# Turning quantised activations and weights by DMA instead of on TensorE in a fused patch-embedding, attention and feed-forward layer

## Chip, cores and metric

The kernel runs on one core of one Trainium2 chip. The metric is the device time of one execution in microseconds (us). A "turn" below is the transposition of a 128 x 768 bf16 tile as six blocks of 128 x 128.

## The reference

The reference takes 64 images of 49 patches with 768 values each and does three things.

1. Tokens: each patch row is RMS-normalised and quantised to 8-bit integers, multiplied by a ternary weight (768 to 256), and a class token and a position vector are added: `h` is 64 x 50 x 256.
2. Attention: the layer norm of `h` goes through three attention passes of 16 heads of width 16, each with its own q, k, v and output weights, a causal mask, a softmax and a layer norm. Their outputs are joined, projected to 256, normalised and added to `h`.
3. Feed-forward: the layer norm of `h` is quantised with one scale for the whole tensor, multiplied by 8-bit gate and up weights (256 to 704), `silu(gate) * up` is quantised again and multiplied by the 8-bit down weight.

```python
xn = patches * rsqrt(mean(patches**2) + 1e-6)
s  = 127.0 / clip(max(abs(xn)), 1e-5)
proj = einsum('bnd,od->bno', clip(round(xn * s), -128, 127) / s, ternary(weight))
```

## The kernel before

The 64 images are worked on in 8 groups (`GROUPS`) of 8 images, each as 4 pairs (`PAIRS`) of two images. Pairs are counted through, n = 0 to 31. One pair fills 128 partitions: one image in rows 0 to 63, the other in rows 64 to 127.

A pair's way to the token matmul is a chain over the engines. SP loads the two images into one of two buffers `x_in` (step `sums` on SP). ACT and DVE take the sum of squares and the largest value (`sums`), DVE makes the scale (`scale`). ACT writes the scaled and shifted values to `x_t`, and DVE subtracts the constant and writes bf16 integers to `x_q` (`shift`, L1083). TensorE turns `x_q` with six 128 x 128 transpositions into a PSUM bank (`turn_q`, L1287), ACT copies the bank to `x_qT` (`turn_q`, L746), and TensorE multiplies `x_qT` by the token weight in six matmuls (`embed`, L1296). DVE scales the product into `hidden` (`embed`, L1104). `x_q` and `x_qT` are single buffers.

Four more units ("chunks" 0 to 3, n = 32 to 35) bring the gate and up weights of the feed-forward stage along the same way during the last group: they are loaded into `x_in`, quantised through `x_t` into `x_q`, turned on TensorE and copied by ACT into `wgT` (L743). Two more chunks hold the down weight, and are turned in another place.

The rest of a group is attention. TensorE makes k and q (L1314) and v (`v`, L1330 and L1333), the scores in 12 units a group (`scores`, L1349 and L1358), turns the probabilities (`turn_p`, L1373), multiplies them by v (`heads`, L1383) and projects (`project`, L1394 and L1399). Most of these go through four PSUM banks `ps_w` used in turn: a step waits until the step four fills earlier has been read.

The order of all steps is written out by hand in the table `AT`. It lists for each engine at which position it does step number i of a kind. Each engine walks its list in that order and waits on semaphores inside a step. PE has 594 steps, ACT 637, DVE 813, POOL 457 and SP 41. Groups overlap: pairs of the next group are embedded while the attention of this one runs. What counts as the position of a step below is its number in its engine's list.

After the attention comes the feed-forward stage, which has its own fixed loops.

Of the kernel before, what the change touches and what calls it, by code (L numbers as in the profile page):

```python
# [32 lines left out]
P = 128  # L33
# [40 lines left out]
    "act": {  # L74
        "sums": (0, 1, 10, 11, 25, 26, 51, 54, 99, 100, 117, 125, 176, 178, 195, 200, 250, 256, 268, 278, 324, 326,
            342, 346, 401, 402, 429, 439, 481, 482, 501, 504,),
        "shift": (2, 5, 13, 15, 33, 39, 61, 71, 106, 113, 137, 145, 185, 188, 205, 213, 260, 266, 283, 289, 332, 338,
            356, 362, 407, 419, 451, 466, 490, 495, 511, 528, 563, 568, 595, 618,),
        "tok_shift": (3,),
        "turn_q": (4, 9, 16, 19, 43, 55, 69, 82, 110, 129, 140, 156, 189, 209, 221, 232, 265, 277, 292, 298, 337,  # L80
            358, 367, 376, 421, 445, 460, 471, 496, 508, 527, 538, 577, 593, 611, 635,),
        "tok_copy": (6, 7,),
        "q_hi": (8,),
        "k_hi": (12,),
        "v_cut": (14, 18, 36,),
        "small": (17,),
        "wv_hi": (20,),
        "turn_x": (21, 22, 23, 24, 93, 95, 97, 98, 170, 171, 172, 173, 244, 246, 247, 248, 319, 321, 322, 323, 397,
# [23 lines left out]
        "fold_hi": (57, 62, 63,),  # L112
        "y_spread": (64,),
        "heads": (67, 70, 89, 90, 118, 135, 139, 158, 159, 167, 196, 206, 220, 227, 239, 240, 271, 279, 301, 307,
            314, 318, 351, 357, 372, 381, 389, 395, 420, 438, 447, 458, 459, 468, 498, 518, 519, 536, 537, 546, 576,
            582, 599, 600, 612, 620, 626, 633,),
        "project": (73, 76, 80, 84, 101, 115, 116, 124, 126, 127, 138, 147, 148, 149, 164, 165, 166, 174, 175, 201,
# [1680 lines left out]
```

## Time and profile before

| | |
|---|---|
| median of 3 runs | 771.42 us (769.8 to 774.2) |
| profiled execution, its own time | 769.84 us |
| its span | 768.1 us |
| busy: PE, DVE, ACT, POOL | 89%, 84%, 76%, 68% of the span |
| token set-up and first group's start | 0 to about 48 us |
| attention stage | about 48 to 660 us |
| hand-over and feed-forward stage | about 660 to 768 us |

Busy time of TensorE counts modelled ends of pipelined matmuls, so a busy engine isn't at its peak; what an operation costs there is read from the distance of one start to the next. Waits are inferred from semaphore events. The windows of the profile give the busy time of each engine in a stretch of the span.

### The profile page before, as it was taken

What the parts mean: (1) busy time and instruction counts of PE and PEld (TensorE: products, weight loads), DVE (VectorE), ACT (ScalarE), POOL (GpSimd) and SP (SyncE); (2) the same over time, 40 slices, a digit from 0 to 9 for tenths busy, and PEclk for the clock granted to TensorE, in tenths of its full rate; (3) what the DMA queues carried; (4) which work ended last, traced back from release to release, by engine and by line L of the source; (5) the groups of instructions that cost most, each with busy time, mean ns of one, the idle gap of its engine ahead of it and who ended that gap; (6) DMA issues with size and microseconds to landing.
All of it is one profiled execution on the core that took longest, in us unless ns stands there. A gap on an engine that the chain in (4) does not pass through costs nothing. (4 is left out here: it accounts for less than half of the span.)

```text
span 768.1 us, 25770 instructions
## 1 busy us (share of the span) xinstructions
PE 684.5 (89%) x9862; PEld 535.2 (70%) x9862; DVE 641.9 (84%) x1395; ACT 584.3 (76%) x1280; POOL 520.0 (68%) x793
## 2 busy tenths in 40 slices
PE   0498799999999999999999999999999999568866
PEld 0277678777877787877877787788778777334455
DVE  4788876899889988989898899889987898759947
ACT  3567888687788678869778878688868887379875
POOL 3459965957687859877677789478948786521154
PEclk9979999999999999999999999999999999869979
DMA  8301000000000000101000000100100000000005
GB/s 240 100 28 33 17 19 17 19 18 20 4 32 27 10 2 34 34 2 33 18 19 3 16 19 3 34 18 18 41 3 22 20 22 22 1 1 1 0 24 148
DMA packets 14980, 21.95 MB, mean 29 GB/s; under 512 B 1992, under 2 KB 11466, under 8 KB 14860
## 3 DMA queue, kind: packets, MB, share of 16 engines
q1 hardware_dynamic: 14424, 19.91, 8.4%
q8 instruction: 80, 1.31, 0.7%
q10 hardware_dynamic: 436, 0.40, 0.4%
q14 instruction: 40, 0.33, 0.1%
HBM read 17.03 MB, written 3.28 MB: 26 GB/s over the span
## 5 line engine op out<-in xcount | busy, mean ns | idle before, releaser
L905 POOL TENSOR_TENSOR k_bd<-kT,rmask 128x400 f32<-128x400 f32 x192 | 167.8, 902 | 7.5 <-PE ps_s L1358 4.3
L806 ACT COPY pT<-ps_w 25x400 f32<-25x400 f32 x192 | 94.8, 494 | 9.2 <-PE ps_w L1373 6.7
L1399 PE MATMUL ps_w<-oy_hi,o_hi 128*128 128x512 f32 x192 | 94.9, 494 | 0.0
L914 POOL TENSOR_TENSOR prob_hi<-prob_hi,rsum 128x800 f32<-128x800 f32 x48 | 74.9, 1559 | 13.3 <-DVE rsum L1151 13.3
L1134 DVE TENSOR_REDUCE nmax<-ps_s 128x16 f32<-128x400 f32 x96 | 72.4, 765 | 11.6 <-PE ps_s L1358 11.3
L786 ACT COPY v_bd<-ps_w 50x256 f32<-50x256 f32 x192 | 70.4, 367 | 13.2 <-PE ps_w L1333 10.9
L1399 PE MATMUL ps_w<-oy_hi,o_lo 128*128 128x512 f32 x192 | 76.3, 397 | 0.0
L1399 PE MATMUL ps_w<-oy_lo,o_hi 128*128 128x512 f32 x192 | 76.2, 397 | 0.0
L827 ACT ACTIVATE ps_w<-ps_w 128x256 f32<-128x256 f32 x96 | 35.6, 371 | 51.7 <-PE ps_w L1399 50.3
L1358 PE MATMUL ps_s<-k_bd,qT 64*25 64x200 f32 (+1 forms) x3072 | 70.5, 291 | 0.0
L919 POOL TENSOR_TENSOR ln<-ln,ln_eps 128x1 f32<-128x1 f32 x96 | 19.9, 208 | 74.6 <-ACT ps_w L827 74.1
L1314 PE MATMUL ps_w<-xh_dense,qk_hi 128*128 128x400 f32 x192 | 68.5, 357 | 1.5 <-DVE xl L1126 1.1
L1314 PE MATMUL ps_w<-xl,qk_hi 128*128 128x400 f32 x192 | 67.2, 350 | 0.0
L1314 PE MATMUL ps_w<-xh_dense,qk_lo 128*128 128x400 f32 x192 | 66.2, 345 | 0.0
L1333 PE MATMUL ps_w<-wv_hi,xh 128*128 128x256 f32 x192 | 61.9, 322 | 0.0
L921 POOL TENSOR_TENSOR ln<-ln,neg_half 128x1 f32<-128x1 f32 x96 | 54.4, 567 | 7.5
L914 POOL TENSOR_TENSOR prob_lo<-prob_lo,rsum 128x400 f32<-128x400 f32 x48 | 42.5, 886 | 19.5 <-DVE rsum L1151 19.5
L1373 PE MATMUL ps_w<-pack,prob_hi 128*128 128x128 f32 x384 | 51.7, 277 | 2.9 <-DVE acc L1169 1.0
L1333 PE MATMUL ps_w<-wv_lo,xh 128*128 128x256 f32 x192 | 54.0, 281 | 0.0
L1333 PE MATMUL ps_w<-wv_hi,xl 128*128 128x256 f32 x192 | 53.7, 280 | 0.0
L1373 PEld LDWEIGHTS ps_w<-pack,prob_hi 128*128 128x128 f32 x384 | 42.1, 141 | 11.1 <-issue 6.5
L813 ACT COPY pT<-ps_w 128x400 f32<-128x400 f32 x96 | 43.3, 506 | 8.1 <-PE ps_w L1373 7.3
(237 smaller groups left out, 2070.4 us busy)
## 6 DMA issues: line engine op xcount, KB each, us to landing
x_in<-in_x SPq DMA_DIRECT2D x64, 147.0 KB
out<-hidden SPq DMA_DIRECT2D x14, 200.0 KB
pT<-in_tok_w SPq DMA_DIRECT2D x1, 768.0 KB, 6.5
hidden<-in_wq SPq DMA_DIRECT2D x1, 768.0 KB, 8.6
k_bd<-in_wk SPq DMA_DIRECT2D x1, 768.0 KB, 9.5
v_bd<-in_wv SPq DMA_DIRECT2D x1, 768.0 KB, 9.2
hidden<-in_wout SPq DMA_DIRECT2D x1, 768.0 KB, 9.3
hidden<-in_wo SPq DMA_DIRECT2D x1, 768.0 KB, 10.8
```

Source lines behind the costliest of these rows:

```text
L786: last = nc.scalar.copy(v_bd[row:row + L, s % 2, b::2, :, e * HD:(e + 1) * HD], v_ps[src:src + L, :, e])
L806: last = nc.scalar.copy(pT[ROWB * h:ROWB * h + LQ, s % 2, c::2, :, 0:LQ], ps_w[row:row + LQ, bank].rearrange("p (j t) -> p j t", j=4)[:, : ...
L813: nc.scalar.copy(pT[:, s % 2, 4 * a:4 * a + 4, :, LQ:L], ps_w[:, bank].rearrange("p (j t) -> p j t", j=4)[:, :, 0:QB * LQ].rearrange("p j ...
L905: last = nc.gpsimd.tensor_tensor(k_bd[:, v % KBD, c], kT[:, w % 2, c, 2 * p * L:(2 * p + 2) * L].unsqueeze(1).broadcast_to([P, HR, 2 * L]) ...
L914: nc.gpsimd.tensor_tensor(pr, pr, rsum[:, s % 2, e].unsqueeze(2).broadcast_to([P, H, WIDTH[e]]), ALU.mult).then_inc(prob_ready, 1)
L921: nc.gpsimd.tensor_tensor(ln2[:, v, 2:3], ln2[:, v, 1:2], neg_half[:, 0:1], ALU.pow).then_inc(r2_ready, 1)
L1134: nc.vector.tensor_reduce(top, s_ps, AX.X, ALU.max, negate=True).then_inc(max_ready, 1)
L1314: mm = nc.tensor.matmul(G[:, 0:GT], wt[:, w, q, k, c * P:(c + 1) * P], xt[:, k, :, 0:L], start=(t == 0), stop=(t == 3 * KC - 1))
L1333: mm = nc.tensor.matmul(cols, xt[:, k, two].rearrange("p b t -> p (b t)"), wt[:, w, k], start=False, stop=(k == KC - 1 and xt is xl))
L1358: mm = nc.tensor.matmul(ps_s[32 * b:32 * b + LQ, e, r, c * HR * W:(c + 1) * HR * W], qT[rows, w % 2, c, first:first + LQ], k_bd[rows, v % ...
L1373: mm = nc.tensor.transpose(G[:, j * P:(j + 1) * P], flat[:, (4 * a + j) * P:(4 * a + j + 1) * P], pack[:])
L1399: mm = nc.tensor.matmul(G[:], ot[:, s % 2, c, 2 * (p % 2):2 * (p % 2) + 2].rearrange("p b t -> p (b t)"), wt[:, w, c], start=False, stop=( ...
```

## The change

For pairs 4 to 31 and for weight chunks 0 to 3 (n = 32 to 35), the six transpositions on TensorE and the copy on ACT go away. SP has a new kind of step, `turn_d`: it waits until `x_q` is written and, for a pair, until the token matmul of the pair before has read `x_qT`. Then it issues six DMAs with `transpose=True`, each of which turns 128 x 128 bf16 from `x_q` in SBUF straight into `x_qT` (pairs) or `wgT` (chunks). All count up one semaphore `xqT_turned`, 16 each. The next `shift` on DVE and the token matmul on TensorE wait for the full count of all six. The four pairs of the first group are turned on TensorE and copied by ACT as before.

The table `AT` is new for every engine: PE has 562 steps (32 fewer), ACT 605 (32 fewer), DVE 813, POOL 457 and SP 73 (32 more). Steps of all kinds have other positions.

```diff
@@ AT @@
     "sp": {
-        "sums": (0, 1, 5, 6, 7, 8, 9, 10, 11, 12, 13, 14, 15, 16, 17, 18, 19, 20, 21, 22, 23, 24, 25, 26, 27, 28, 29,
-            30, 31, 32, 33, 34, 35, 36, 37, 38, 39, 40,),
-        "weights": (2, 3, 4,),
+        "sums": (0, 1, 4, 5, 7, 8, 10, 11, 14, 15, 17, 19, 23, 24, 25, 27, 31, 32, 34, 35, 38, 39, 42, 43, 45, 48,
+            49, 51, 55, 56, 58, 59, 62, 63, 65, 67, 70, 71,),
+        "weights": (2, 3, 6,),
+        "turn_d": (9, 12, 13, 16, 18, 20, 21, 22, 26, 28, 29, 30, 33, 36, 37, 40, 41, 44, 46, 47, 50, 52, 53, 54, 57,
+            60, 61, 64, 66, 68, 69, 72,),
     },
...
@@ pe @@
-        "turn_q": (1, 3, 8, 10, 29, 41, 58, 67, 94, 108, 123, 138, 167, 185, 197, 206, 241, 252, 264, 272, 308, 326,
-            334, 346, 387, 411, 424, 436, 459, 467, 489, 499, 538, 552, 571, 591,),
+        "turn_q": (1, 3, 7, 9,),
-        "embed": (5, 6, 9, 12, 40, 48, 64, 73, 102, 118, 135, 152, 170, 189, 203, 214, 246, 256, 267, 286, 322, 331,
-            345, 356, 390, 423, 435, 439, 463, 475, 496, 504,),
+        "embed": (5, 6, 8, 11, 34, 42, 53, 73, 97, 107, 118, 139, 163, 185, 198, 208, 231, 252, 267, 275, 300, 313,
+            328, 345, 370, 382, 404, 409, 436, 446, 464, 481,),
...
@@ sync @@
             def do(step):
                 kind, m = step[0], step[-1]
+                if kind == "turn_d":
+                    n = PAIRS + step[1]
+                    c = ffn_chunk(n // PAIRS, n % PAIRS)
+                    sp.wait_ge(xq_ready, n + 1)
+                    if c is None:
+                        bank, fill = bank_of(("embed", (n - 1) % PAIRS, (n - 1) // PAIRS))
+                        sp.wait_ge(filled[bank], fill)
+                        dst = x_qT[:]
+                    else:
+                        dst = wgT[:, c // 2, 3 * (c % 2):3 * (c % 2) + 3].rearrange("p f k t -> p (f k) t")
+                    for j in range(PC):
+                        sp.dma_start(dst[:, j], x_q[:, j * P:(j + 1) * P], transpose=True).then_inc(xqT_turned, 16)
...
             for b in (0, 1):
                 sp.wait_ge(x_loaded[b], 64 * GROUPS + 96)
+            sp.wait_ge(xqT_turned, 16 * PC * PAIRS * GROUPS)
...
@@ scalar, turn_q @@
-                    c = ffn_chunk(m, p)
-                    if c is not None:
-                        w_ps = ps_w[:, bank, 0:PC * P // 2].bitcast(BF16)
-                        dst = wgT[:, c // 2, 3 * (c % 2):3 * (c % 2) + 3].rearrange("p f k t -> p (f k t)")
-                        nc.scalar.copy(dst, w_ps).then_inc(xqT_ready, 1)
-                        return
...
@@ vector, shift @@
-                    need(dve, xqT_ready, n)
+                    need(dve, xqT_ready, min(n, PAIRS))
+                    need(dve, xqT_turned, 16 * PC * (n - PAIRS))
...
@@ tensor, embed @@
-                    pe.wait_ge(xqT_ready, PAIRS * m + p + 1)
+                    if m == 0:
+                        pe.wait_ge(xqT_ready, p + 1)
+                    else:
+                        pe.wait_ge(xqT_turned, 16 * PC * (PAIRS * (m - 1) + p + 1))
```

## Rows read from the trace of the kernel before

**Rows 1.** The page's first part: busy time, share and instructions of each engine.

```profile
PE 684.5 (89%) x9862; PEld 535.2 (70%) x9862; DVE 641.9 (84%) x1395; ACT 584.3 (76%) x1280; POOL 520.0 (68%) x793
```

**Rows 2.** Windows: stretch, length, busy time (instructions) by engine, clock, DMA share, GB/s.

```profile
276.00:352.00 76.00, 75.33 (x1171) 60.91 (x1170) 66.60 (x157) 61.90 (x146) 59.49 (x99) 1.00 0.06 18
...
504.00:580.00 76.00, 74.48 (x1167) 60.25 (x1166) 67.75 (x157) 59.51 (x140) 57.20 (x92) 1.00 0.07 20
...
sum 612.00, PE 590.52 PEld 475.60 DVE 530.77 ACT 487.02 POOL 464.82; mean PE 73.81 PEld 59.45 DVE 66.35 ACT 60.88 POOL 58.10
```

**Rows 3.** Windows from 660 us to the end of the span, same columns.

```profile
660.00:674.00 14.00, 4.94 (x14) 3.30 (x14) 9.43 (x29) 1.69 (x6) 7.18 (x19) 0.77 0.00 0
674.00:768.00 94.00, 68.76 (x470) 43.92 (x470) 70.97 (x95) 73.14 (x134) 29.79 (x29) 0.88 0.13 36
```

**Rows 4.** Timeline of PE, 299 to 318 us: start, length, instructions merged.

```profile
299.89 0.92 PE L1383 MATMUL ps_w<-pT,v_bd 128*32 128x50 f32 x64
300.74 0.66 PE L1373 MATMUL ps_w<-pack,prob_lo 128*128 128x128 f32 x4
...
311.42 0.51 PE L1287 MATMUL ps_w<-id,x_q 128*128 128x128 bf16 x6
311.77 1.04 PE L1373 MATMUL ps_w<-pack,prob_hi 128*128 128x128 f32 x8
312.65 0.27 PE L1330 MATMUL ps_w<-bias,ones 96*128 96x256 bf16 x1
...
314.32 0.83 PE L1296 MATMUL ps_w<-tokT,x_qT 128*128 128x256 bf16 x6
314.98 0.60 PE L1373 MATMUL ps_w<-pack,prob_lo 128*128 128x128 f32 x4
...
316.21 1.09 PE L1373 MATMUL ps_w<-pack,prob_hi 128*128 128x128 f32 x8
317.23 0.27 PE L1349 MATMUL ps_s<-mask,pick 64*128 64x200 bf16 x2
```

**Rows 5.** Groups by line, ACT's copies: busy us, mean ns, idle before.

```profile
L746 ACT COPY x_qT<-ps_w 128x768 bf16<-128x768 bf16 x32 | 25.5, 797 | 4.8 <-DVE ln L1107 4.1 <-PE ps_w L1287 0.4
...
L743 ACT COPY wgT<-ps_w 128x768 bf16<-128x768 bf16 x4 | 3.2, 803 | 0.7 <-PE ps_w L1287 0.7
```

**Rows 6.** Waits of PE, 50 to 650 us: total us, times, longest.

```profile
PE ps_s L1349 <- DVE prob_lo L1138: 1.8, 1, 1.8
...
PE ps_w L1330 <- ACT x_qT L746: 1.4, 1, 1.4
```

**Rows 7.** Line L1287 as an instruction group: ns min/median/max, starts, forms.

```profile
L1287 PE MATMUL ps_w<-id,x_q x216: 216/219/314, 16.8 to 659.7; 128*128 128x128 bf16 x108
```

**Rows 8.** Timeline of DVE: the `shift` of n = 4 and of n = 35.

```profile
60.76 1.21 DVE L1083 TENSOR_SCALAR x_q<-x_t 128x768 bf16<-128x768 f32 x1
...
645.53 0.55 DVE L1083 TENSOR_SCALAR x_q<-x_t 128x768 bf16<-128x768 f32 x1
```

**Rows 9.** DMA issue on SP, 100 to 600 us: ns min/median/max of one.

```profile
L631 SPq DMA_DIRECT2D x_in<-in_x x44: 268/271/845, 131.4 to 519.1; - x44
```

**Rows 10.** Issues on SP at the start: start, length, and one's us to landing.

```profile
4.06 0.63 SPq L607 DMA_DIRECT2D hidden<-in_head_mask  x1
...
id<-in_ident SPq DMA_DIRECT2D x1, 64.0 KB, 7.2
```

**Rows 11.** Windows of 1 us behind the `x_q` that ended at 308.8 us.

```profile
308.00:309.00 1.00, 1.00 (x7) 0.96 (x6) 0.97 (x4) 0.69 (x3) 0.33 (x2) 1.00 0.00 0
309.00:310.00 1.00, 1.00 (x8) 1.00 (x7) 1.00 (x2) 1.00 (x3) 0.92 (x3) 1.00 0.21 31
310.00:311.00 1.00, 1.00 (x7) 1.00 (x6) 1.00 (x3) 1.00 (x2) 1.00 (x2) 1.00 0.33 123
311.00:312.00 1.00, 1.00 (x13) 0.83 (x12) 1.00 (x4) 1.00 (x3) 1.00 (x2) 1.00 0.43 164
312.00:313.00 1.00, 1.00 (x11) 0.99 (x10) 0.87 (x4) 1.00 (x3) 1.00 (x2) 1.00 0.00 0
```

**Rows 12.** Waits of SP's queue over the span.

```profile
SPq L631 <- DVE x_q L1083: 480.9, 29, 43.5
```

More of the change, by code:

```diff
@@ L73 @@
     },
     "act": {
[L75 to L81, printed above, removed]
@@ L112 @@
[L112 to L117, printed above, removed]
[4 rows of a table removed]
+        "sums": (0, 1, 10, 11, 26, 27, 42, 48, 93, 94, 118, 120, 166, 167, 186, 188, 239, 244, 257, 260, 307, 313,
+            332, 340, 383, 385, 403, 408, 453, 459, 472, 478,),
@@ new lines @@
+        "tok_shift": (2,),
+        "shift": (3, 5, 14, 15, 31, 36, 49, 77, 101, 110, 127, 135, 172, 177, 199, 212, 247, 253, 279, 289, 321, 330,
+            346, 365, 388, 395, 425, 430, 464, 469, 484, 502, 530, 539, 550, 567,),
+        "small": (4,),
+        "turn_q": (6, 12, 16, 17,),
+        "tok_copy": (7, 8,),
+        "q_hi": (9,),
+        "k_hi": (13,),
+        "v_cut": (18, 20, 37,),
+        "wv_hi": (19,),
+        "turn_x": (21, 23, 24, 25, 89, 90, 91, 92, 161, 162, 163, 164, 232, 234, 235, 238, 303, 304, 305, 306, 378,
+            380, 381, 382, 448, 449, 451, 452, 520, 521, 523, 527,),
@@ new lines @@
+        "wo_hi": (35,),
+        "soft": (43, 44, 50, 51, 63, 64, 69, 70, 85, 97, 103, 104, 111, 112, 122, 124, 132, 133, 143, 145, 156, 158,
[4 rows of a table added]
+        "y_spread": (47,),
+        "z_cut": (53, 65, 71,),
+        "v": (54, 55, 66, 73, 86, 87, 136, 137, 147, 148, 159, 160, 206, 208, 218, 220, 229, 233, 271, 272, 286, 287,
+            301, 302, 350, 351, 358, 359, 375, 379, 419, 420, 431, 440, 441, 450, 495, 496, 503, 509, 517, 518, 553,
+            558, 579, 583, 593, 594,),
+        "turn_p": (56, 57, 58, 62, 74, 75, 79, 82, 108, 109, 116, 117, 128, 129, 138, 141, 144, 149, 150, 151, 181,
[4 rows of a table added]
@@ L122 @@
+        "fold_hi": (60, 67, 72,),
+        "heads": (61, 68, 83, 84, 114, 123, 139, 146, 155, 157, 184, 194, 210, 211, 228, 231, 261, 263, 280, 285,
+            299, 300, 333, 338, 354, 355, 368, 376, 402, 410, 424, 432, 439, 447, 470, 487, 500, 501, 514, 516, 540,
+            557, 566, 574, 582, 592, 595, 602,),
+        "project": (76, 78, 80, 81, 88, 95, 96, 119, 121, 130, 131, 134, 142, 152, 153, 154, 165, 178, 179, 192, 195,
[4 rows of a table added]
     },
     "pool": {
-        "sums": (0, 1, 3, 4, 12, 13, 28, 32, 55, 57, 69, 75, 111, 112, 126, 127, 166, 167, 179, 186, 219, 220, 232,
-            234, 275, 277, 301, 305, 334, 335, 345, 359,),
@@ new lines @@
+        "embed": (4, 5, 9, 10, 33, 50, 52, 53, 93, 99, 100, 104, 129, 147, 160, 161, 192, 197, 216, 218, 250, 253,
+            263, 277, 294, 318, 324, 325, 357, 378, 380, 381,),
+        "k_lo": (6,),
+        "v_left": (7, 15,),
+        "turn_x": (8, 16, 32, 42, 49, 55, 75, 78, 119, 154, 157, 158, 191, 193, 196, 200, 273, 274, 304, 305, 311,
+            331, 347, 352, 375, 395, 411, 412, 427, 434, 435, 445,),
+        "spread": (13, 14, 17, 18, 19, 20, 25, 30, 36, 37, 41, 51, 60, 61, 64, 65, 66, 69, 70, 85, 86, 87, 97, 98,
[4 rows of a table added]
@@ L159 @@
[L159 to L163 removed]
+        "tok_sum": (0,),
+        "sums": (1, 3, 12, 13, 32, 33, 45, 63, 115, 116, 143, 144, 213, 214, 235, 239, 314, 322, 332, 339, 408, 416,
+            437, 449, 509, 510, 535, 540, 605, 610, 630, 639, 694, 714, 715, 742, 796, 797,),
@@ L164 @@
+        "tok_unit": (2,),
+        "scale": (4, 5, 14, 15, 34, 35, 48, 90, 119, 125, 150, 162, 217, 222, 246, 260, 321, 327, 338, 358, 414, 419,
+            448, 460, 513, 514, 557, 567, 611, 622, 633, 659,),
+        "id_cast": (6,),
+        "shift": (7, 9, 17, 19, 37, 44, 59, 91, 123, 133, 159, 171, 219, 230, 259, 284, 323, 330, 371, 381, 418, 433,
+            457, 485, 517, 529, 568, 579, 618, 627, 654, 674, 712, 721, 750, 789,),
         "tok_clip": (8,),
         "consts": (10,),
-        "embed": (11, 16, 23, 26, 60, 69, 93, 102, 138, 159, 182, 209, 229, 260, 277, 291, 334, 349, 366, 385, 437,
-            451, 468, 482, 532, 580, 594, 598, 626, 644, 674, 683,),
@@ L214 @@
-        "sig": (499,),
+        "embed": (11, 16, 20, 23, 53, 65, 80, 102, 138, 155, 172, 203, 233, 267, 287, 298, 333, 361, 385, 396, 428,
+            453, 476, 497, 533, 550, 585, 589, 631, 643, 671, 693,),
+        "q_lo": (18,),
+        "o_centre": (21,),
+        "norm_x": (22, 25, 26, 28, 97, 105, 106, 107, 200, 201, 202, 206, 295, 297, 300, 303, 383, 392, 399, 400,
+            487, 496, 500, 503, 591, 593, 596, 597, 677, 690, 691, 696,),
+        "y_row": (24,),
+        "x_lo": (27, 29, 30, 31, 108, 110, 113, 114, 207, 209, 210, 211, 301, 307, 309, 312, 401, 402, 403, 405, 504,
+            505, 506, 507, 599, 600, 603, 604, 695, 697, 699, 706,),
@@ new lines @@
+        "b_centre": (36,),
+        "wv_lo": (38,),
+        "max": (39, 41, 46, 47, 66, 67, 71, 74, 89, 100, 111, 112, 129, 131, 139, 140, 157, 158, 173, 177, 189, 194,
[4 rows of a table added]
+        "soft": (40, 42, 49, 50, 68, 69, 78, 79, 96, 101, 120, 121, 130, 132, 142, 146, 160, 161, 176, 180, 191, 197,
[4 rows of a table added]
+        "y_scale": (43,),
+        "bo_col": (51,),
+        "sum": (52, 57, 60, 61, 75, 76, 82, 83, 103, 122, 126, 127, 134, 135, 151, 152, 163, 170, 178, 184, 199, 205,
[4 rows of a table added]
+        "z_row": (54, 55,),
+        "over": (56, 58, 62, 64, 77, 84, 85, 86, 104, 124, 128, 136, 141, 145, 153, 154, 165, 179, 181, 185, 204,
[4 rows of a table added]
@@ new lines @@
+        "o_lo": (70,),
+        "fold_lo": (72, 81, 88,),
+        "heads": (73, 87, 98, 99, 137, 149, 174, 186, 196, 198, 234, 247, 272, 274, 294, 299, 340, 342, 368, 373,
+            393, 394, 438, 445, 469, 470, 483, 499, 532, 542, 563, 573, 586, 595, 626, 649, 666, 667, 684, 688, 722,
+            746, 754, 765, 780, 794, 795, 804,),
+        "project": (92, 93, 94, 95, 109, 117, 118, 147, 148, 164, 166, 168, 182, 192, 193, 195, 216, 226, 227, 245,
[4 rows of a table added]
+        "mix": (156, 167, 169, 183, 254, 262, 263, 275, 350, 356, 357, 379, 452, 459, 464, 465, 553, 554, 565, 584,
[3 rows of a table added]
@@ L215 @@
+        "sig": (511,),
     },
@@ new lines @@
+        "beta": (10,),
+        "wo_turn": (12, 17, 45,),
+        "turn_x": (13, 14, 15, 16, 74, 78, 79, 80, 143, 144, 145, 147, 209, 213, 214, 215, 278, 279, 282, 283, 348,
[7 rows of a table added]
+        "scores": (24, 25, 31, 32, 41, 46, 49, 52, 58, 60, 76, 77, 91, 92, 99, 100, 109, 110, 120, 121, 127, 131,
[4 rows of a table added]
+        "bo_turn": (33,),
+        "y_spread": (35,),
+        "bo_fold": (37, 38,),
+        "v": (39, 40, 54, 59, 71, 72, 115, 116, 128, 129, 140, 141, 183, 184, 192, 195, 206, 210, 245, 246, 258, 259,
+            276, 277, 320, 321, 326, 327, 343, 347, 385, 386, 395, 406, 407, 413, 456, 457, 465, 469, 479, 480, 512,
+            517, 536, 541, 550, 551,),
@@ new lines @@
+        "turn_p": (43, 44, 47, 51, 61, 62, 65, 68, 90, 93, 98, 101, 108, 111, 117, 123, 125, 130, 132, 133, 158, 161,
[4 rows of a table added]
+        "fold": (48, 56, 57,),
+        "heads": (50, 55, 69, 70, 95, 104, 119, 126, 137, 138, 164, 171, 189, 190, 204, 207, 236, 237, 255, 256, 273,
+            274, 304, 306, 324, 325, 337, 344, 366, 376, 389, 396, 405, 412, 432, 449, 462, 463, 476, 477, 503, 518,
+            525, 533, 540, 549, 553, 559,),
+        "project": (63, 64, 66, 67, 75, 81, 82, 102, 103, 112, 113, 114, 124, 134, 135, 136, 148, 155, 156, 169, 172,
[4 rows of a table added]
@@ L264 @@
     "mix": PAIRS, "mix2": PAIRS, "k": NS * KC, "q": NS * KC, "v": S, "heads": S, "spread": V, "project": V,
-    "scores": U, "max": U, "soft": U, "sum": U, "over": U, "turn_p": U,
+    "kbd": S, "scores": U, "max": U, "soft": U, "sum": U, "over": U, "turn_p": U,
 }
```

96 lines of the change are left out of this document (15 added, 81 removed), and 138 rows, old and new, of the table AT.

## The prediction

> **What bounds the kernel now.** I read the page's shares first, then windows of the length of a group, then the waits of the fullest engine, then its timeline around one turn. The shares alone put TensorE first with 89% and DVE second with 84% [rows 1]. The windows show that the mean hides a stage where TensorE is full: in two windows of 76 us, about a group each, it is busy for 75.33 and 74.48 us, with DVE at 66.60 and 67.75 and ACT at 61.90 and 59.51, at a granted clock of 1.00 [rows 2]. Over eight such windows (48 to 660 us) it is busy for 590.52 of 612 us, so 21.5 us are idle [rows 2]. Each wait that remains in this stage is short: the longest is 1.8 us, and one of 1.4 us was for ACT's copy of a turned tile [rows 6]. So in this stage the end is set by the sum of TensorE's work, and each slot taken off TensorE should shorten it. What follows, 660 to 768 us, is another stage that is not touched, except that it needs `wgT`; there TensorE is busy 4.94 of 14 us and 68.76 of 94 us [rows 3].
>
> **What goes from TensorE.** A turn is six transpositions. Each lasts 219 ns by its record [rows 7], but they overlap: six start at 311.42 and the next step starts at 311.77, a slot of 0.35 us [rows 4]. The records' lengths would give 0.51 us a turn [rows 4]; I take the distance of starts, 0.34 to 0.35 us, since a modelled end lies under the next step's start. 28 pairs and 4 chunks make 32 turns, and 32 x 0.34 = 10.9 us. The upper bound is 32 x 0.51 = 16.3 us.
>
> The Trainium skill (VectorE: DVE Perf Modes, section "The three transpose paths") gives 390 ns for a 128 x 128 bf16 transposition on TensorE and 1309 ns for one by DMA. By its first figure 192 transpositions would give back 75 us, an estimate from that page; the rows disagree with it, as six take 0.35 us in a full stream. By its second figure, six in a row would take an estimated 7.9 us, which is taken up among the rivals.
>
> **What goes from ACT.** 28 copies of 0.797 us and 4 of 0.803 us, 25.5 us in all [rows 5]. ACT has some 15 us free in each window of 76 [rows 2], so this is worth nothing by itself. It lets ACT empty banks sooner, and each bank is filled 32 times less in total. The one PE wait that names the copy is 1.4 us [rows 6], and I take that. Bounds: nothing, and a third of TensorE's idle 21.5 us, 7 us [rows 2].
>
> **What is added.** SP issues 192 more DMAs. SP mostly waits: 480.9 us of its time went to waiting for `x_q` before a load [rows 12]. So its own time costs nothing, but what it does between `x_q` and the token matmul does. Call T the time from the end of `shift` to the landing of all six. No row shows a transposing DMA. From below: six issues at the 0.27 us of a plain load [rows 9], 1.6 us, and 1 us until something lands, so about 2.7 us; behind the `x_q` that ended at 308.8 us the bytes of the next load (2 x 147 KB) flow from 309 to 312 us [rows 11], 3 us for 294 KB against the 192 KB of a turn, so bytes are no obstacle. From above: six issues at 0.63 us, the longest of the small loads at the start, and the 7.2 us to landing of a 64 KB load among many [rows 10], 11 us. At neither end does a stage like this stand: the queue is nearly empty here (share 0.06) [rows 2], which draws it to the lower end, and turning may cost more issue and more transfer than copying, which draws it up. I take 6 us.
>
> **What waits for a turn.** Behind a late turn stand the token matmul on TensorE, with every later step of its list, and the next `shift` on DVE, with every later step of that list. What cover has a turn? DVE's steps from `shift` of n = 4 (position 42 before, start 60.76) to that of n = 35 (position 788, 645.53) take 584.8 / 746 = 0.78 us each [rows 8]. In the new lists DVE has k steps between `shift` of a pair and its own `embed` step, which must come after TensorE's. Taken off are about 0.6 us for the `shift` itself and 0.9 us for the matmuls, so the cover is 0.78k - 1.5. The smallest k are 10 (n = 16, 20, 27), 11 (7), 12 (23), 13 (10, 28), 14 (12, 15, 18), 15 (8, 19) and 16 (4, 24, 29); 10 gives 6.3 us, 11 gives 7.1, 12 gives 7.9 and 13 gives 8.7. The chain of `x_qT` has a cover too: `turn_d` of n waits for the matmul of n - 1, and between the token matmuls of 26 and 27 the new list has only `heads`, two `v` and one `turn_p`. With 0.85, 2 x 1.67 and 1.02 us by the distances of starts [rows 4] that is 5.2 us. The next smallest are 7.4 us (18 to 19), 7.5 (4 to 5) and 8.3 (5 to 6) by the same sort of sum. On SP's list a load of two images stands just ahead of some turns and is set free by the same `x_q`: of those above before n = 7, 8, 12, 19, 24 and 29. Its 3 us of bytes [rows 11] overlap the six issues, so I add 2 us to T for these.
>
> Stalls by T then:
> - T = 6: n = 27 lacks 0.8 us, n = 7 (8 against 7.1) 0.9 us; 1.7 us in all.
> - T = 8: n = 16 and 20 lack 1.7 each, 27 2.8, 7 2.9, 12 0.5, 19 0.6, 5 0.5; about 11 us.
> - T = 9: about 21 us.
> - T = 11: 16 and 20 4.7 each, 27 5.8, 7 5.9, 12 3.5, 5 3.5, 23 3.1, 8 and 19 2.8 to 3.6 each, and eight smaller ones; about 51 us.
>
> So the decision lies near T = 8 us.
>
> Loads move too. A load behind a `turn_d` in SP's list is kept until that turn is issued; the shortest distance to the step that reads it is 9 DVE steps (7 us) for n = 15, 18 and 19, and 3 for chunk 34, against 3 us of bytes and up to 3.8 us of issues [rows 10, 11]. DVE then loses up to 2 us near the end once, and has over 8 us free in each window [rows 2]; nothing. At the end, `turn_d` of n = 35 is the last step on SP; its `shift` has 23 steps behind it on DVE, some 18 us, which hides T.
>
> **Sum.** -10.9 (TensorE) - 1.4 (bank wait) + 1.7 (stalls at T = 6) = -10.6 us. From the profiled execution's own 769.84 us that is 759.2; it stands 1.6 us under the median of the runs, 771.42, which gives 760.8. I predict 761 us.
>
> **Rivals.** What can be told from no change is 0.5%, about 3.9 us: 767.6 to 775.3 us.
>
> - Turning fits its cover (T up to 7.3 us), forecast: 753 to 767 us. For it: TensorE without waits, a nearly empty DMA queue. Chance 0.60.
> - The gain is used up: T of 7.3 to 8.5 us, or the new lists leave some 8 us more idle time on TensorE in places that have nothing to do with turning (the 21.5 us are 2.7 a window, and every step has been moved; DVE, busy 67 of 76 us, has little room to catch up). 769.84 - 10.9 + 8 is 767, on the median 769; 768 to 775 us. Chance 0.16.
> - Slower, one mechanism: the six DMAs don't overlap, so that each adds its own whole turn to T. With 1.5 us each T is 9, and 21 us of stalls less 12.3 give +9, 780 us; at 11 us it is +39, 810 us. It decides from 1.4 us each. For it: nothing in the trace shows a turning DMA, and small ones pay mostly a fixed cost (0.27 us of issue for a load and 0.63 us for one of 4 KB [rows 9, 10]). Against it: the loads' issues overlap their bytes [rows 11]. The skill's 1309 ns, if the six follow one another, puts an estimated 7.9 us at the very point of decision, a stall of some 10 us and an estimated time of about 770. Chance of a slower kernel 0.24.
> - That the change doesn't do what it says: the transpositions do go from TensorE's list, so this has no chance of its own.
>
> **Range.** The low end is the 10.9 us and the 7 us of idle time given back, 753 us on the median. The high end takes in T = 9 us, 780 us, and 2 us for the lists, 782 us; above it are T over 9 us, about 0.13, and below 753 about 0.05. The likeliest case alone has 753 to 767 us. Faster 0.60, within 0.5% 0.16, slower 0.24.
>
> **What the new profile would show.** L1287 only 24 times on PE, L746 4 times, L743 gone. Six issues per turn on SP: at 0.3 to 0.5 us each the forecast holds, at over 1 us it fails. T between 5 and 7 us. The waits of PE: the token matmul of n = 27 and of n = 7 among the few waits for a DMA, below 3 us in total. TensorE busy in the windows of the attention stage as fully as now, 97 to 98%, with the stage 10 to 12 us shorter, and the feed-forward stage as long as now, about 94 us. The prediction is wrong if the waits for `x_qT` add up to over 5 us, if many PE waits on other engines grow, or if the slot of a turn wasn't 0.34 us in most places.

## The result and the profile after

| | before | after |
|---|---|---|
| median | 770.79 us (4 runs, 769.8 to 774.2) | 819.61 us (4 runs, 815.17 to 826.21) |
| ratio, 95% interval | | 1.0632 [1.054, 1.0724] |
| profiled execution, span | 769.84, 768.1 us | 815.17, 813.4 us |

The change makes the kernel 49 us slower. The forecast was 761 us, 753 to 782.

I read the page first: busy time by engine, the granted TensorE clock in 40 slices, and the DMA packets.

```profile
PE 693.8 (85%) x9670; PEld 538.8 (66%) x9670; DVE 650.8 (80%) x1395; ACT 562.0 (69%) x1248; POOL 518.6 (64%) x793
...
PEclk9979999999999999999899999898999999959979
...
DMA packets 45701, 28.26 MB, mean 35 GB/s; under 512 B 32712, under 2 KB 42186, under 8 KB 45580
```

The 192 matmul records of the turns are gone (9862 to 9670, [rows 1]), yet every engine has a smaller share of a longer span. The clock has slices of 8 in the middle. Then the windows, to find the stage:

```profile
48.00:648.00 600.00, 548.43 (x8128) 438.22 (x8128) 488.18 (x1085) 419.17 (x966) 418.54 (x641) 0.96 0.11 28
...
276.00:352.00 76.00, 69.49 (x1050) 56.45 (x1050) 64.98 (x143) 53.81 (x127) 54.26 (x88) 0.96 0.13 35
504.00:580.00 76.00, 65.94 (x940) 51.67 (x940) 56.97 (x135) 47.27 (x112) 49.33 (x83) 0.91 0.11 28
719.00:813.40 94.40, 69.59 (x470) 44.31 (x470) 70.99 (x95) 73.23 (x134) 29.79 (x29) 0.86 0.13 36
```

The last row answers to the last of [rows 3]: the feed-forward stage still takes 94 us. So all of the loss lies in the attention stage, which ends at about 705 us in place of 660. In the windows of [rows 2] TensorE was busy for 75.33 and 74.48 us at a clock of 1.00; now it is 69.49 us at 0.96 and 65.94 us at 0.91. The waits of 50 to 700 us name what is late:

```profile
POOL ln L927 <- ACT ps_w L835: 103.7, 56, 8.7
ACT ps_w L835 <- PE ps_w L1411: 55.4, 53, 5.9
PEld ps_w L1308 <- DMA x_qT<-x_q: 36.5, 16, 5.2
PE ps_w L1308 <- DMA x_qT<-x_q: 32.3, 15, 4.8
DVE x_q L1092 <- DMA x_qT<-x_q: 23.0, 8, 4.5
```

The same two first rows of the kernel before, 50 to 660 us:

```profile
POOL ln L919 <- ACT ps_w L827: 69.5, 48, 7.6
ACT ps_w L827 <- PE ps_w L1399: 45.7, 50, 2.1
```

The token matmul (L1308) waits 32.3 us in 15 pairs for its turn and the next `shift` (L1092) 23.0 us in 8. I had named a sum over 5 us as what would refute the forecast. The largest waits of the token matmul were 4.8 us at n = 20, 4.3 at 23, 3.9 at 28 and 3.4 at 16. POOL and ACT had long waits in the kernel before too; they are 34 and 10 us longer now, in turn, for what TensorE does late. Why a turn takes so long is in the issue rows of SP's queue (ns min/median/max):

```profile
L616 SPq DMA_TRANSPOSE x_qT<-x_q x168: 1093/1232/2590, 54.5 to 609.6; - x168
L616 SPq DMA_TRANSPOSE wgT<-x_q x24: 1093/1233/2695, 628.6 to 699.8; - x24
```

A load held the queue for 0.27 us [rows 9]; a transposing DMA holds it for 1.23 us, and the six of a turn stand in one queue. The timeline of one turn, n = 8, on SP, DVE and PE:

```profile
134.26 0.62 SPq L644 DMA_DIRECT2D x_in<-in_x  x2
134.97 8.54 SPq L616 DMA_TRANSPOSE x_qT<-x_q  x6
...
133.60 0.62 DVE L1092 TENSOR_SCALAR x_q<-x_t 128x768 bf16<-128x768 f32 x1
...
144.73 1.46 PE L1308 MATMUL ps_w<-tokT,x_qT 128*128 128x256 bf16 x6 [2.99 <-DMA x_qT<-x_q]
```

`x_q` is ready at 134.22. The load takes 0.7 us, six issues 8.54 us, and the matmul that waits for the last starts 1.2 us later: T is 10.5 us. Without a load ahead it is shorter: at n = 10 `x_q` is ready at 163.67 and the waiting token matmul starts at 172.38, so T is 8.7 us; at n = 16 and n = 20 it is 9.6 and 9.7 us.

A wait has a second price. At n = 16 TensorE stands still from 301.4 to 304.75 us; here is PE's timeline, and then windows of 1 us:

```profile
304.75 1.12 PE L1308 MATMUL ps_w<-tokT,x_qT 128*128 128x256 bf16 x6 [3.35 <-DMA x_qT<-x_q]
305.67 1.06 PE L1385 MATMUL ps_w<-pack,prob_lo 128*128 128x128 f32 x4
```

```profile
303.00:304.00 1.00, 0.00 (x0) 0.00 (x0) 0.00 (x0) 0.00 (x0) 0.00 (x0) 1.00 0.15 33
...
306.00:307.00 1.00, 1.00 (x7) 1.00 (x6) 0.29 (x1) 0.00 (x0) 0.00 (x0) 0.50 0.51 192
307.00:308.00 1.00, 1.00 (x6) 1.00 (x5) 0.51 (x1) 0.51 (x1) 0.00 (x0) 0.50 0.49 95
308.00:309.00 1.00, 1.00 (x37) 0.48 (x35) 0.88 (x4) 0.99 (x4) 0.31 (x1) 0.72 0.42 160
```

From 303 to 304 us no engine works. When TensorE runs again, its clock is at 1.2 GHz (0.50) for about 3 us: the six matmuls take 1.12 us and the four behind them 1.06 us, where they took 0.83 and 0.60 to 0.66 us at 2.4 GHz [rows 4].

### The profile page after: what moved, and what is told of

It is laid out like the page before. It is cut to its first block and busy times, and to the rows that moved or that the text cites. A ratio compares the mean times of both kernels' runs of the same rounds, so it can differ in the third digit from the quotient of the medians.

```text
span 813.4 us, 25514 instructions
## 1 busy us (share of the span) xinstructions
PE 693.8 (85%) x9670; PEld 538.8 (66%) x9670; DVE 650.8 (80%) x1395; ACT 562.0 (69%) x1248; POOL 518.6 (64%) x793
## 5 line engine op out<-in xcount | busy, mean ns | idle before, releaser
L913 POOL TENSOR_TENSOR k_bd<-kT,rmask 128x400 f32<-128x400 f32 x192 | 164.8, 887 | 6.0 <-ACT kT L774 4.7
L814 ACT COPY pT<-ps_w 25x400 f32<-25x400 f32 x192 | 94.6, 492 | 12.3 <-PE ps_w L1385 10.0
L1370 PE MATMUL ps_s<-k_bd,qT 64*25 64x200 f32 (+1 forms) x3072 | 72.8, 296 | 1.5 <-issue 1.5
L1326 PE MATMUL ps_w<-xh_dense,qk_hi 128*128 128x400 f32 x192 | 70.2, 366 | 1.2 <-DVE xl L1135 0.8
L1308 PE MATMUL ps_w<-tokT,x_qT 128*128 128x256 bf16 x192 | 32.5, 316 | 37.7 <-DMA x_qT<-x_q 32.3
L1385 PE MATMUL ps_w<-pack,prob_hi 128*128 128x128 f32 x384 | 54.6, 287 | 4.8 <-DVE acc L1178 3.4
L1385 PEld LDWEIGHTS ps_w<-pack,prob_hi 128*128 128x128 f32 x384 | 45.1, 147 | 13.5 <-issue 5.5
```

Source lines behind the costliest of these rows:

```text
L814: last = nc.scalar.copy(pT[ROWB * h:ROWB * h + LQ, s % 2, c::2, :, 0:LQ], ps_w[row:row + LQ, bank].rearrange("p (j t) -> p j t", j=4)[:, : ...
L913: last = nc.gpsimd.tensor_tensor(k_bd[:, v % KBD, c], kT[:, w % 2, c, 2 * p * L:(2 * p + 2) * L].unsqueeze(1).broadcast_to([P, HR, 2 * L]) ...
L1326: mm = nc.tensor.matmul(G[:, 0:GT], wt[:, w, q, k, c * P:(c + 1) * P], xt[:, k, :, 0:L], start=(t == 0), stop=(t == 3 * KC - 1))
L1370: mm = nc.tensor.matmul(ps_s[32 * b:32 * b + LQ, e, r, c * HR * W:(c + 1) * HR * W], qT[rows, w % 2, c, first:first + LQ], k_bd[rows, v % ...
L1385: mm = nc.tensor.transpose(G[:, j * P:(j + 1) * P], flat[:, (4 * a + j) * P:(4 * a + j + 1) * P], pack[:])
```

## The experiments

All runs are single-core, each with runs of the kernel before on the same chip; "before" is their median (770.8 to 772.4 us). They fall into two questions. First: what makes a turn slow, its bytes, its number of DMAs, or the lists? Second, once that was known: where are the 10.9 us that TensorE was to save?

### The number of DMAs in a turn (e1, e2, e5, e6)

e1 issues only the first of six DMAs for each pair (five sixths of `x_qT` keep old values), e2 the first four (a third keeps old values); chunks keep all six.

```diff
-for j in range(PC):
+for j in range(1 if c is None else PC):     # e1; 4 in e2
```

> The changed kernel, but of each pair's turn only the first of the six DMAs is issued for pairs 4 to 31 (so five of six blocks of x_qT keep old data; the weight chunks are turned whole). In the changed kernel one transposing DMA keeps SP's queue for 1.23 us (median of 168) and a turn takes 9 to 10.5 us from x_q to the token matmul. Theory A (the length of a turn is the cause: waits of TensorE for x_qT, 32.3 us, and stretches at half clock behind them): a turn takes 2.5 to 3 us here, no wait for x_qT is left, no half clock in the attention stage, and the time is 757 to 764 us. Theory B (the new lists of steps are themselves worse): still over 785 us. Theory C (turning DMAs slow the other engines by using SBUF beside them): a part of the loss stays in proportion to the DMAs, about a sixth of 48 us, 8 us, so 767 to 772 us.

> As e1, with four of the six DMAs for each pair (two blocks keep old data). A turn should take about 4 x 1.3 + 1.2 = 6.4 us, close to the 6 us that the prediction took. Theory A: the prediction's table of stalls gives 2 to 4 us for it, so 761 to 766 us, waits of TensorE for x_qT below 4 us. Theory B: over 785 us. Theory C: two thirds of the 48 us stay, about 800 us.

e5 turns the same data as one DMA of 128 x 768, and e6 as twelve of 64 x 128.

```diff
-for j in range(PC):
-    sp.dma_start(dst[:, j], x_q[:, j * P:(j + 1) * P], transpose=True).then_inc(xqT_turned, 16)
+sp.dma_start(dst, x_q[:], transpose=True).then_inc(xqT_turned, 16)                                  # e5
+for j in range(PC):                                                                                 # e6
+    for r in (0, 64):
+        sp.dma_start(dst[:, j, r:r + 64], x_q[r:r + 64, j * P:(j + 1) * P], transpose=True).then_inc(xqT_turned, 16)
```

> The changed kernel, but each turn is issued as one transposing DMA of 128 x 768 into the six blocks instead of six DMAs of 128 x 128. If the 1.23 us that SP spends on each transposing DMA is a fixed price of an instruction, a turn takes about 1.3 + 1.5 = 3 us here, SP is free after 1.3 us, and the time is that of e1, 770 to 778 us. If the price goes with the blocks of data that SP writes descriptors for, SP is kept for about 7 us as before and the time stays at 810 to 825 us.

> The changed kernel with twelve transposing DMAs a turn, each of 64 rows by 128 columns, so half the data each. Fixed price of an instruction: 1.2 us each, a turn of 15 us and a time of 860 us or more. Price by data: 0.6 us each, and a time within 10 us of 819.

| DMAs a pair | size of each | time | ratio to before |
|---|---|---|---|
| 1 (e1) | 128 x 128 | 774.45 us | 1.0025 [0.9992, 1.0058] |
| 1 (e5) | 128 x 768 | 776.65 us | 1.0064 [1.0028, 1.01] |
| 4 (e2) | 128 x 128 | 790.65 us | 1.0234 [1.0187, 1.0282] |
| 6 (the change) | 128 x 128 | 819.61 us | 1.0632 [1.054, 1.0724] |
| 12 (e6) | 64 x 128 | 1008.28 us (one run) | 1.308 |

The issue rows, first of e1 and then of e5 with their us from issue to landing, then of e6 with PE's wait for it:

```profile
L624 SPq DMA_TRANSPOSE x_qT<-x_q x28: 1093/1095/2242, 54.1 to 564.4; - x28
...
DMA to landing us min/median/max: 2.3/2.9/5.2
```

```profile
L615 SPq DMA_TRANSPOSE x_qT<-x_q x28: 1210/1212/2170, 54.0 to 564.2; - x28
...
DMA to landing us min/median/max: 2.8/3.6/5.8
```

```profile
L617 SPq DMA_TRANSPOSE x_qT<-x_q x336: 1088/1228/2486, 54.5 to 794.8; - x168
```

```profile
PE ps_w L1309 <- DMA x_qT<-x_q: 185.5, 25, 11.8
```

One transposing DMA holds the queue for 1.1 to 1.2 us, whether it turns 64 x 128, 128 x 128 or 128 x 768. The price is one for each instruction. The same 192 KB, in one DMA, land 3.6 us after the issue, in place of 9.8 us for six at n = 8 (134.97 to 144.73 us); the waits of PE and of DVE then name `x_qT` no more, and 43 of the 49 us are back, with the lists and everything else as in the change. This settles the main cause. It also answers theories B and C: the lists are the change's own and the bytes are all moved, and the time is 776.65 us.

Two of the times were missed. e1 was expected at 757 to 764 us and took 774.45: the late turns are gone and the forecast's gain still doesn't show. e2 was expected at 761 to 766 us with waits below 4 us and took 790.65. Its shortest turns have the T of 6.2 us that I had reckoned with (`x_q` ready at 162.47, token matmul at 168.65, n = 10), one behind a load 8.2 us (n = 8), and yet these waits stand in its list:

```profile
PE ps_w L1316 <- DMA x_qT<-x_q: 9.6, 8, 2.6
DVE x_q L1100 <- DMA x_qT<-x_q: 7.6, 4, 2.6
```

So even with about the T of the forecast this kernel is 19.7 us slower than before.

The Trainium skill (VectorE: DVE Perf Modes, section "The three transpose paths") gives 1309 ns for 128 x 128 by DMA. The 1.23 us from issue to issue is near it for blocks of that size in a row, but one alone lands 2.9 us after its issue (e1). For 128 x 768 a price by the block would be an estimated 7.9 us, and 3.6 us are measured. So that figure isn't to be multiplied by blocks when one DMA can turn them all.

### The lower clock (e3)

e3 is the change with 12 to 41 idle matmuls on TensorE, into the bank that the token matmul then overwrites, ahead of each of the eleven latest token matmuls, to keep the clock up while it waits.

```diff
+for c in range(FILL.get(PAIRS * m + p, 0)):
+    nc.tensor.matmul(G[:, 0:D], tokT[:, c % PC, 0:P], tokT[:, c % PC], start=True, stop=True)
```

> The changed kernel with all six DMAs; ahead of the 11 token matmuls that waited 1.5 us or more, TensorE does throw-away matmuls of 256 columns into the same bank, as many as fill the wait (12 to 41 of 0.11 us). The wait stays as long, TensorE is only kept at work in it. Theory A with the clock as a second part: the half-clock stretches behind the waits (47.8 us of the attention stage are at half clock, none before the change) go, and the time falls by 12 to 24 us, to 795 to 807 us. If the clock costs nothing (the waits and lists alone explain all), the time stays within 4 us of 819 us.

Measured: 814.01 us, ratio 1.0551 [1.049, 1.0612]. Windows as above:

```profile
276.00:352.00 76.00, 70.80 (x1082) 57.50 (x1081) 64.79 (x144) 54.40 (x126) 54.01 (x87) 1.00 0.13 35
504.00:580.00 76.00, 67.58 (x938) 53.93 (x937) 56.09 (x132) 45.56 (x109) 47.45 (x80) 0.98 0.11 28
```

The clock is back at 1.00 and 0.98 (0.96 and 0.91 without), and the time is 5.6 us lower by the medians, but the two intervals overlap: taken together they leave room for anything from nothing to some 15 us. The 12 to 24 us that I expected didn't show. Since one DMA a turn gives back 43 us, the clock is no main cause.

### Which part the lists have (e4, e7, e8)

e4 has the new lists with every turn put back on TensorE and ACT by a rule: for pairs `turn_q` three steps before its token matmul or sooner, the copy soon behind it. e7 and e8 have the old lists with `turn_q` of n from 4 on taken out and `turn_d` put into SP's list; e7 with one of six DMAs for pairs (five sixths of `x_qT` keep old values), e8 with all six.

> The new lists, but all turns on TensorE and ACT again, as before the change: turn_q is put back on PE's list three steps ahead of each token matmul and on ACT's list behind it, no transposing DMA is issued. Theory A: the new lists are about as good as the old ones, 768 to 778 us. Theory B (the lists are the cause): 795 us or more.

> The lists of before with turn_q of pairs 4 to 31 and of the chunks taken out of PE's and ACT's list, turned by DMA, and only the first of six blocks turned for pairs (e1's shortening; five blocks of x_qT keep old data). SP does the turn ahead of the load of pair n + 2, or behind it where that load is needed soon. Theory A with the lists as a second part: e1 lost 14 us against the forecast through the new lists, and here the forecast's saving of 10.9 us shows: 758 to 765 us. If the lists weren't the cause of e1's missing gain, this gives 770 to 778 us too, and the 0.34 us of a turn aren't worth what they were counted at.

> As e7, with all six DMAs of every turn. The lists of before leave 3 DVE steps of cover at n = 12, 7 at n = 28, 9 at n = 16 and 27, against 10 and more in the new ones. If the new lists give cover, this is slower than the changed kernel, 825 to 850 us; if their cover is worth nothing and they only cost 14 us, it is 800 to 812 us.

Measured: e4 807.21 us, 1.046 [1.0413, 1.0507]; e7 772.43 us, 1.0011 [0.9992, 1.0031]; e8 843.76 us, 1.0924 [1.0887, 1.0962]. Waits of e8:

```profile
DVE x_q L1120 <- DMA x_qT<-x_q: 48.9, 9, 10.3
PE ps_w L1337 <- DMA x_qT<-x_q: 46.2, 10, 8.1
```

With six DMAs the new lists are 24 us better than the old ones, so they do give a turn more cover. e4 came out where "the lists are the cause" had it (795 us or more), but e5 has the same lists at 776.65 us. It has new waits of its own (ACT's copy waited 22.2 us for the turn put so close ahead of it), so it shows the price of my placement, not of the lists. e7 raised the second question: TensorE and ACT are freed of the turns, and still it isn't faster. It isn't free of late turns, though:

```profile
DVE x_q L1128 <- DMA x_qT<-x_q: 9.3, 4, 4.7
PE ps_w L1345 <- DMA x_qT<-x_q: 2.5, 1, 2.5
```

So e7 alone can't tell a gain that isn't there from one that these waits eat up; the next three runs can, since they have no turn by DMA.

### What a slot of TensorE is worth (e9, e10, e11)

These and the next five are the kernel before with its own lists. For pairs 4 to 31, e9 does the transpositions twice; e10 copies only 128 of 768 columns on ACT; e11 copies 128 columns and does one of six transpositions.

```diff
-for c in range(PC):
+for c in ([*range(PC)] * 2 if PAIRS <= PAIRS * m + p < PAIRS * GROUPS else range(PC)):   # e9; range(1) in e11
```

> The kernel before, its lists and its ACT copies unchanged, with TensorE doing each turn of pairs 4 to 31 twice into the same bank (12 transpositions in place of 6). This adds 28 slots of 0.34 us, 9.5 us, to TensorE. Theory A (TensorE's sum sets the end of the stage, my prediction's first step): about 9.5 us slower, 780 us. Theory B (TensorE is one of several engines that are near their limit, its slots are worth only part of their length): 1 to 5 us slower, 772 to 776 us. If the slot of six is longer than 0.34 us, the distance of starts in the profile will show it.

> The kernel before with ACT's copy of a turned tile cut to its first 128 of 768 columns for pairs 4 to 31 (so x_qT keeps old blocks there: the output is not the reference's). TensorE's work is unchanged. ACT is relieved of some 28 x 0.6 = 17 us and the token matmul can start 0.6 us sooner. My prediction: 1.4 us faster at most (the one bank wait). Rival: ACT's copies are on chains that matter, and the time falls by 4 us or more.

> The kernel before with one of six transpositions on TensorE and one of six blocks in ACT's copy, for pairs 4 to 31 (the rest of x_qT keeps old values: the output is not the reference's). TensorE is relieved of 28 x 5/6 x 0.34 = 8 us, ACT of 17 us; no step moves and no DMA is added. Theory A (TensorE's sum sets the end): 8 us faster, 763 us. Theory B (the freed slots turn into idle time, since DVE, ACT and the chains between them hold the pace): within 3 us of the kernel before. If A holds here while the one-block DMA kernels stayed at 772 to 775 us, the DMA's own wait eats the gain; if B holds, the gain of 10.9 us was never there.

| | starts taken by the 28 turns on TensorE | time | ratio |
|---|---|---|---|
| before | 10.7 us | 771.37 us | |
| e9 | 20.2 us | 774.13 us | 1.004 [1.0018, 1.0062] |
| e10 | not changed | 771.88 us | 1.0006 [0.9983, 1.0029] |
| e11 | 4.1 us | 770.96 us | 1.0 [0.9979, 1.0021] |

The second column is the sum, over 28 turns, of the distance from a turn's first start to the next step's first start in PE's timeline, less the idle time that the timeline shows between them. The 10.7 us are 0.38 us a turn, a little over the 0.34 us of the forecast. But 9.5 us more cost 2.8 us, and 6.5 us less gave nothing. The page of e11 and its window show how that hides:

```profile
PE 684.3 (89%) x9722; PEld 529.6 (69%) x9722; DVE 642.6 (84%) x1395; ACT 570.1 (74%) x1280; POOL 520.2 (68%) x793
```

```profile
276.00:352.00 76.00, 74.93 (x1152) 59.81 (x1152) 67.30 (x158) 59.64 (x146) 58.37 (x95) 1.00 0.06 18
```

140 matmuls are gone, yet PE's busy time is 684.3 us against 684.5 [rows 1], and the window is as full as in [rows 2]. The likely reason, not tried by itself, is that the modelled ends of the matmuls reach over short waits, so that a TensorE that waits a little after many steps looks 97 to 99% busy.

### Who holds the pace (e13 to e17)

e13 does DVE's subtraction of `shift` twice, e14 on 128 of 768 columns; e15 does ACT's copy twice; e16 cuts TensorE's turn, ACT's copy and DVE's shift all to one block; e17 adds two reductions on DVE behind `embed` that nothing waits for.

```diff
+nc.vector.tensor_scalar(x_q[:], x_t[:], MAGIC, None, ALU.subtract)   # e13: once more, with a drain
-nc.vector.tensor_scalar(x_q[:], x_t[:], MAGIC, None, ALU.subtract).then_inc(xq_ready, 1)
+nc.vector.tensor_scalar(x_q[:, 0:w], x_t[:, 0:w], MAGIC, None, ALU.subtract).then_inc(xq_ready, 1)   # e14: w = 128
+nc.vector.tensor_reduce(spare[:, i:i + 1], hidden[:, n, :], AX.X, ALU.max)   # e17: i = 0, 1
```

> The kernel before with DVE's subtraction of shift (0.55 us) done twice, with a drain between, for pairs 4 to 31: 28 x 0.55 us, some 15 us more for DVE, nothing more for TensorE. If DVE holds the pace of the attention stage: 12 to 18 us slower, 783 to 789 us. If the pace is shared by all the engines' chains, as TensorE's doubled turns (9.5 us added, 2.8 us slower) suggest: 3 to 6 us slower. If DVE's free time takes it: within 2 us.

> The kernel before with DVE's subtraction of shift cut to its first 128 of 768 columns for pairs 4 to 31 (the rest of x_q keeps old values: the output is not the reference's): some 28 x 0.4 = 11 us less for DVE, nothing less for TensorE. If DVE holds the pace: 8 to 11 us faster, 761 to 763 us. If the pace is shared: 0 to 4 us faster.

> The kernel before with ACT's copy of a turned tile done twice for pairs 4 to 31: 28 x 0.8 us, 22 us more for ACT, and x_qT 0.8 us later each time. ACT has some 15 us free in each window of 76. If ACT's free time takes it, as my prediction has it for the copies removed: within 2 us. If the chains through ACT matter: 5 us slower or more.

> The kernel before with TensorE's turn, ACT's copy and DVE's shift all cut to one of six blocks for pairs 4 to 31 (the output is not the reference's): 8 us less for TensorE, 17 for ACT, 11 for DVE. If TensorE and DVE hold the pace in turns, so that only both together give something: 5 to 9 us faster, 762 to 766 us. If the order of steps and the small tiles' chains hold it: within 3 us of the kernel before.

> The kernel before with two more reductions on DVE (128 x 256 to a spare column, some 0.39 us each) behind the embed step of pairs 4 to 31: 28 x 0.78 us, 22 us more for DVE, on no chain that anything else waits for, and with nothing added to the way of x_q. It tells whether DVE's time or the longer way of x_q made e13 (22 us more of DVE's busy time, 15.4 us slower) slow. If DVE's time: 12 to 18 us slower. If it was the way of x_q (or a conflict of shift with POOL): within 6 us.

| | busy time changed on the pages | time, before | ratio |
|---|---|---|---|
| e13 | DVE +24.8, POOL +6.7 us | 787.87, 772.44 us | 1.02 [1.0173, 1.0227] |
| e17 | DVE +16.4 us | 782.21, 772.18 us | 1.0133 [1.0093, 1.0174] |
| e15 | ACT +19.0 us | 782.01, 772.44 us | 1.0117 [1.0085, 1.0149] |
| e14 | DVE -6.8, POOL -6.6 us | 768.67, 772.44 us | 0.9945 [0.9921, 0.997] |
| e16 | PE -4.9, ACT -15.2, DVE -9.1, POOL -7.2 us | 763.93, 772.44 us | 0.9885 [0.9857, 0.9912] |

The groups that were added, e13 and then e17:

```profile
L1084 DVE TENSOR_SCALAR x_q<-x_t 128x768 bf16<-128x768 f32 x28 | 22.3, 795 | 5.5 <-ACT x_t L733 3.0 <-ACT x_qT L746 2.3
```

```profile
L1113 DVE TENSOR_REDUCE spare<-hidden 128x1 f32<-128x256 f32 x56 | 19.9, 397 | 0.0
```

19.9 us of DVE work off every chain cost 10.0 us, 22.3 us on the way of `x_q` cost 15.4 us, and 19 us of ACT's cost 9.6 us; 9.5 us of TensorE's cost 2.8 us. So half to two thirds of DVE's and half of ACT's added time show in the end, and some three tenths of TensorE's: no engine alone holds the pace. Taking from one gives little or nothing (0 us for ACT or for TensorE with ACT, 3.8 us for DVE, which relieves POOL too), taking from all three gives 8.5 us. These cuts also shorten the way of `x_q` and `x_qT`, so e16 doesn't tell the engines' time from the length of that way. e15 can't tell ACT's time from the 0.8 us by which it delays `x_qT`; e17 can for DVE, since nothing waits for what it adds.

### Old lists with one DMA a turn (e12, e18)

e12 has the old lists and one DMA of 128 x 768 for all 32 turns. e18 leaves n = 4, 5, 12, 16, 20 and 28 on TensorE and ACT.

> The old lists with all 32 turns as one transposing DMA of 128 x 768 each, TensorE's transpositions and ACT's copies of them gone; the output is the reference's. The new lists with the same DMA took 776.65 us. T is about 3.4 + 1.2 us against some 1.5 us of the turn on TensorE and ACT. Theory A (lists don't matter at this T, TensorE's 10.9 us are gained): 760 to 765 us. Theory B (old lists have too little cover for a T of 4 to 5 us; the one-block runs on either list were at 772 to 774): 775 to 790 us.

> The old lists with one transposing DMA of 128 x 768 for 22 pairs and the four chunks, and TensorE and ACT for n = 4, 5, 12, 16, 20 and 28, whose turns by DMA DVE's next shift waited for (11.0 us in four waits); the output is the reference's. If those waits made the 5 us that the old lists with one DMA lost: 770 to 772 us, no change against before. If TensorE's and ACT's freed time is worth something once no turn is late: 766 to 769 us. If a turning DMA costs something in itself: 774 us or more.

Measured: e12 776.68 us, 1.0072 [1.0045, 1.0099]; e18 773.85 us, 1.003 [1.001, 1.005]. DVE's wait in e12, which is gone from e18's list:

```profile
DVE x_q L1119 <- DMA x_qT<-x_q: 11.0, 4, 5.1
```

Against the before of each, e12 is 5.3 us slower and e18 1.7 us, so some 3.6 of the 5.3 us went with the four late turns; the intervals just meet. e18 still is 0.3% above before, between the two expected cases (770 to 772, and 774 or more) and under the 0.5% that I take as telling. No version with turns by DMA beats the kernel before.

## Why the prediction was wrong

**The step that failed first: T.** "Six issues at the 0.27 us of a plain load" was the lower end, and between 2.7 and 11 us I took 6. A turning DMA's issue was on no row. Its measured price is 1.23 us (1.42 us on the mean at n = 8), the last lands 1.2 us behind its issue, and a load ahead adds 0.7 us: T is 8.7 to 10.5 us. The rival for a slower kernel had this mechanism, with a time of 780 us at T = 9 and 810 at 11; I gave it 0.24. The point of decision, T near 8 us, was also right, but it was reached at 1.23 us a DMA and not only at 1.4. The estimate of 7.9 us for six, from the 1309 ns of the Trainium skill (VectorE: DVE Perf Modes, section "The three transpose paths"), was the best single hint, and lay 0.8 us under the smallest T.

**The table of stalls.** Its sum came out: at T of 8.7 to 10.5 us it gives some 18 to 44 us, and PE waited for `x_qT` 32.3 us. Pair by pair it didn't. It put n = 7 and n = 27 first, with 3.9 and 3.8 us at a T of 9; they waited 0.2 and 2.2 us. The longest waits were at n = 20 and 23, of which 23 was to wait 1.1 us. The covers were worked out from one mean pace of DVE, and they count one step too many (between `shift` and `embed` of n = 16 there are 9 steps and not 10). In part the sum is luck, and at the T of e2 it failed: 2 to 4 us expected, 9.6 us measured.

**The second step: TensorE's slots.** The slot was sized nearly right (10.9 us forecast for 32 turns; 10.7 us measured for 28). Its worth was not: I took "the end is set by the sum of TensorE's work" from a busy time of 97%. e9 and e11 show 2.8 us for 9.5 us added and 0.4 us, within the noise, for 6.5 us removed. So the -10.9 us of the sum is about 0, and the same holds for the -12.3 us that I took off the slower rival. With the table's 18 to 44 us of stalls and no gain it would have said 789 to 815 us; 819.6 were measured.

**What was right.** The turn stayed on TensorE for the first four pairs only. Of my signs, issues of over 1 us and waits for `x_qT` of over 5 us said that the forecast fails, and both came. ACT's copies are worth nothing by themselves (e10: 0.5 us slower, within its interval). The cover from the lists is real (24 us, e8 against the change). The feed-forward stage is unmoved, and bytes are no obstacle (e5 moves the same bytes).

**What I left out.** The clock, which was in no term: 0.96 on the mean of 48 to 648 us against 1.00, which makes about 48 us at half clock. By e3 it is worth 5.6 us, which isn't clear of the noise.

**The account.** 43 us of the 49 go with the number of DMAs a turn (change to e5). The remaining 5.9 us (e5 against before) stand where my sum had -12.3, and their cause stays open. They aren't late turns, since nothing in e5 waits for `x_qT`. e12, with the old lists and the same DMA, takes the same time (776.65 and 776.68 us), but for another reason in part: there DVE waits 11.0 us and TensorE 2.9 us for turns, and without four of them (e18) 1.7 us of the loss are left. So the new lists may well cost some 4 us of their own, which the equal times hide; the intervals of e5 and e18 overlap. The granted clock from 48 to 648 us is 0.99 in e5, e12 and e18 and 1.00 before, and no run tried what that costs.

## What to carry over

Before moving work to DMAs, count instructions on the issuing queue and price each by its kind; if a kind isn't on the trace, take a price that decides against you as likely, measure it first, and look whether one instruction can do the whole. A nearly full busy row of TensorE doesn't prove that its sum sets the end: the cheap test is to double the disputed work in the unchanged kernel and see how much of it shows. In this kernel, whose order is balanced by hand, adding to an engine cost three tenths to two thirds of it, and taking from TensorE and ACT gave nothing until DVE got less too.

## What the runs showed of the chip

- A transposing DMA holds SP's queue for 1.09 to 1.23 us at the median, at 64 x 128, 128 x 128 and 128 x 768 bf16 alike; a plain load of 147 KB held it 0.27 us [rows 9].
- From SBUF to SBUF 128 x 768 lands 3.6 us after its issue, against 2.9 us for 128 x 128 alone (e1).
- DVE's f32 to bf16 subtraction of 128 x 768 lasts 0.49 to 1.61 us in e13 (median 0.68), and its second pass raised POOL's busy time by 6.7 us; cutting it (e14) lowered POOL's by 6.6 us. e17's reductions, 19.9 us of DVE time, moved POOL's by 0.2 us only. So it looks as if this subtraction and POOL's work hold each other up; no run tried it by itself.
- Six transpositions take a slot of 0.38 us on the mean, twelve 0.72, one 0.15.
